# Two expert stages whose tiles without rows run first instead of last, and a shared fill of spare rows

## The chip, the cores and the metric

The kernel runs on one core of a Trainium2 chip. The metric is the device time of one execution in microseconds (us); lower is better. A core has a matrix engine (TensorE, PE in the profile), a vector engine (VectorE, DVE), an activation engine (ScalarE, ACT), a general one (GpSimd, POOL) and an engine that mostly issues transfers (SyncE, SP). Each runs its own list of instructions in order; they wait for each other through semaphores.

## What is computed

Two layers over x of 32 sequences x 128 tokens x 128 channels, so 4096 tokens, in fp32. Both layers end in a mixture of 8 experts of which each token takes two. Cut to what matters here:

```python
def _L0_ffn_ref(x, Wg, W1, W2, W3, Ws1, Ws2, Ws3):      # layer 0, after a per-sequence linear map
    router = xf @ Wg
    top_logits, idx = jax.lax.top_k(router, K)           # K = 2
    probs = jax.nn.softmax(top_logits.astype(jnp.float32), axis=-1).astype(x.dtype)
    w = jnp.zeros((n, E), x.dtype).at[jnp.arange(n)[:, None], idx].add(probs)
    h = jax.nn.silu(jnp.einsum('tc,ech->eth', xf, W1)) * jnp.einsum('tc,ech->eth', xf, W2)
    y = jnp.einsum('eth,ehc,te->tc', h, W3, w)
    hs = jax.nn.silu(xf @ Ws1) * (xf @ Ws2)
    y = y + (hs @ Ws3).reshape(b, t, c)

def _L1_ffn_ref(x, ...):                                 # layer 1, after a per-sequence adapter
    x = x + o @ w_o + b_o                                # o: attention of 16 heads over each sequence
    h = _layernorm(x, ln2_g, ln2_b).reshape(B * S, D)
    topv, topi = jax.lax.top_k(h @ gate_w + gate_b, TOPK)
    hid = jax.nn.relu(jnp.einsum('td,edf->etf', h, W1) + b1[:, None, :])
    out_e = jnp.einsum('etf,efd->etd', hid, W2) + b2[:, None, :]
    moe = jnp.einsum('etd,te->td', out_e, ew)
    return x + moe.reshape(B, S, D)
```

Expert widths are 176 in layer 0 and 512 in layer 1.

## The kernel before, in words

**Stages.** `layer0` routes the tokens and computes the shared part; `experts0` runs layer 0's experts; `pre_attention` and `attention` follow, the latter with layer 1's router; `experts1` runs layer 1's experts and writes the output. Each stage is a block that ends with a barrier of all engines.

**Rows and tiles.** The router gives each pair of token and expert a place in a buffer in memory (`dispatch_rows` in layer 0, `late_rows` in layer 1), where every expert has a region. GpSimd scatters the token rows there with indirect transfers (`route_scatter`, 64 instructions at L358 for each layer). The experts work on tiles of 256 rows. 39 tiles (`ETILES`) always suffice, whatever the routing; a tile beyond those that the routing needs has no rows of tokens. It reads a zeroed dead area, computes on it, and sends its result to spare rows, so it costs what any tile costs. Which expert and which rows a tile takes stands in an integer table that VectorE computes when the routing is over (`table_counts` L420, `table_experts` L439, `table_rows` L449, `table_sends` L460, `table_end` L474): columns 0 to 38 the expert, 39 to 77 the first row, then, from `DONE`, how many sends each half of the result waits for. `w.tabled` is 1 when the experts are there and 2 when the rows are. Tile t takes place t in the list of tiles by expert, so tiles without rows are the last.

Since a region's last tile may be part empty, its tail is filled with spare rows, each from SyncE (`table_fill` L382, with the tile buffer `m.tail` as source): 8 transfers at L389 in layer 0, behind the routing.

**The start of an expert stage.** The first two tiles (`LEAD`) are loaded by SyncE before the stage's block: `lead_weights` (L835) reads the expert number of each from the table (`value_load`, a read of a table entry into a register) and loads its weights; `lead_rows` (L843) reads two row numbers, waits for the tails and for all scatters to have landed, and loads the rows. GpSimd waits for all scatters too, at the end of the preceding block. In the stage SyncE loads tiles 2 to 38 into 8 buffers (`EB`), for each: two table reads (L997, L998), the rows (L1002; L2008 in layer 1), the weights (L1004; L2010).

**In the stage.** Per tile TensorE turns the rows (L889), ScalarE and VectorE split weights and rows in high and low parts (L913, L921 to L925), TensorE multiplies (L939, then L1040 or L2040), ScalarE or VectorE writes the result (`eo` L1094, `fo` L2051), and GpSimd sends it in two indirect transfers (L948, `send_rows`) to `expert_rows`. There are four result buffers (`OB`), each with a semaphore (`st`) that its sends raise.

**The end of an expert stage.** `expert_rows` holds the result for each token twice, for the lower-numbered and for the higher-numbered of its experts. `fetch_halves` (L857) on SyncE, after all loads, fetches the lower half into `V` and the upper one into `X3` (shown as X<-expert_rows), each in four transfers. Ahead of each `sends_done` (L868) reads from the table, for each of the four result buffers, how many sends have to have landed, and waits. The lower half waits for the tiles of experts 0 to 6, the upper half for all tiles that have rows; neither waits for tiles without rows. VectorE adds them: in layer 0 eight lower sums at L956, once all of `V` is there, the upper ones mostly in the next stage; in layer 1 lower and upper ones in turn at L2078 (each upper one waits for its quarter), with the output behind each pair (L2119).

```python
    for b in range(OB):
        at = DONE + OB * a + b
        sends = sp.value_load(m.table[0:1, at:at + 1], min_val=32 * (8 if a else 4), max_val=32 * 10)
        sp.wait_ge(sent[b], sends + 32 * uses(b, OB) if layer else sends)
        sp.sem_inc(m.passed, 1)
```

Of the kernel before, what the change touches and what calls it, by code (L numbers as in the profile page):

```python
# [11 lines left out]
I32 = mybir.dt.int32  # L12
# [4 lines left out]
P = 128  # L17
# [149 lines left out]
def allocate(m, d):  # L167
# [14 lines left out]
    m.table = m.sb("table", [P, DONE + 2 * OB], I32)  # L182
# [12 lines left out]
    m.filled = m.sem("filled")  # L195
# [10 lines left out]
DONE = 2 * ETILES + E  # L206
HALVES = 4
# [155 lines left out]
class TileTable:  # L363
# [3 lines left out]
    def __init__(self, m, ctx, tag, indexed):  # L367
# [8 lines left out]
        self.real, self.sends = sb("real", [P, 2, OB * 10]), sb("sends", [P, 2, OB])  # L376
        self.is_e, self.val, self.val2 = (sb(x, [P, ETILES, E1]) for x in ("is_e", "val", "val2"))
        self.link, self.ended, self.tabled = m.sems(*(s + tag for s in ("tt_link", "ended", "tabled")))
# [14 lines left out]
def table_sync(w, sp):  # L393


    m = w.m
    sp.dma_start(m.xbufs[0][E * REGION:].rearrange("(e a p) c -> p e a c", a=2, p=P), m.tail[:, E:]).then_inc(w.tails, 16)


FILLS = 2  # L400
# [19 lines left out]
def table_counts(w, dve):  # L420
# [12 lines left out]
    c(v.tensor_tensor(w.excl[:], w.incl[:], w.need[:], ALU.subtract))  # L433

# [4 lines left out]
def table_experts(w, dve):  # L439

    m, v, c = w.m, w.m.nc.vector, w.chain
    tl = m.const[:, C_TILE:C_TILE + ETILES]
    c(v.tensor_tensor(w.cmp[:], bc(w.incl[:, 0:E].unsqueeze(1), P, ETILES, E), bc(tl.unsqueeze(2), P, ETILES, E),
# [5 lines left out]
def table_rows(w, dve):  # L449
# [3 lines left out]
    tl = m.const[:, C_TILE:C_TILE + ETILES]  # L453
    c(v.tensor_tensor(w.is_e[:], bc(w.expert[:].unsqueeze(2), P, ETILES, E1), bc(exps.unsqueeze(1), P, ETILES, E1),
                      ALU.is_equal))
    c(v.scalar_tensor_tensor(out=w.val[:], in0=bc(tl.unsqueeze(2), P, ETILES, E1), scalar=float(SLOTS),
# [3 lines left out]
def table_sends(w, dve):  # L460
# [4 lines left out]
    tl = m.const[:, C_TILE:C_TILE + ETILES]  # L465
# [41 lines left out]
def layer0(m, d):  # L507
# [3 lines left out]
    with ExitStack() as ctx:  # L511
# [17 lines left out]
        rank = psN[:, 1, 2 * (P + E):2 * (P + E) + (GT + 1) * E]  # L529
        r = Router(m, ctx, "0", None, ROW_BUFFERS)  # L530
        tiles = TileTable(m, ctx, "0", r.indexed)
        style_ld, first_ld, next_ld, shared_ld, rest_ld, x_ld = m.sems(
# [7 lines left out]
        with nc.Block(no_gpsimd_drain=True) as block:  # L540
            @block.sync
            def _(sp):
# [19 lines left out]
                lead_rows(m, sp, tiles, 16 * (E + 1),  # L562
                          [(r.scattered[b], r.sends * len(range(b, GROUPS, ROW_BUFFERS))) for b in range(ROW_BUFFERS)],
# [3 lines left out]
            def _(pool):  # L567
# [6 lines left out]
                for b in range(ROW_BUFFERS):  # L574
                    pool.wait_ge(r.scattered[b], r.sends * len(range(b, GROUPS, ROW_BUFFERS)))
# [1607 lines left out]
```

## Time and profile before

| | |
|---|---|
| runs of the kernel | 777.63, 775.84, 770.14 us; median 775.84 |
| the profiled execution | 771.82 us, its span 769.0 us |
| busy in the span | PE 80%, DVE 62%, POOL 56%, ACT 50% |
| stage `layer0` | up to about 133 us |
| `experts0` | about 133 to 281 us |
| `pre_attention` and `attention` | about 281 to 603 us |
| `experts1` | about 603 us to the end |
| sends (L948) | 78 in each expert stage, two for each tile |

Times within the profile are counted from the start of the span. A row of the timeline gives start, busy time, engine, line, operation, what is written from what is read, how many like instructions stand in it, and in brackets how long the engine was idle before it and what ended that. SPq and ACTq rows are transfers as the engine issues them; their time is that of issuing. The time of an indirect send is GpSimd's work to issue it; it lands later.

### The profile page before, as it was taken

The numbers are of one execution on the slowest core, as the hardware profiler recorded it, in microseconds if no ns is written. First come the engines' busy times: TensorE is split into PE (matmuls) and PEld (weight loads), VectorE is DVE, ScalarE is ACT, GpSimd is POOL, SyncE is SP. The second block draws the span as 40 slices with busy tenths as digits, with TensorE's granted clock in tenths as the row PEclk, the third lists the DMA queues.
The fourth block names the chain that finished last, engine by engine and source line by source line (L and its number), as shares of the span: only waits on it lengthen the run. The fifth ranks groups of instructions, "written<-read, shape, count | busy, mean of one in ns | idle before, by whom it ended". The sixth has DMA issues, their size and how long they took to land.

```text
span 769.0 us, 17719 instructions
## 1 busy us (share of the span) xinstructions
PE 617.8 (80%) x5541; PEld 490.0 (64%) x5541; DVE 474.6 (62%) x1520; ACT 383.4 (50%) x838; POOL 431.3 (56%) x573
## 2 busy tenths in 40 slices
PE   5797885977778648875999999999972499999882
PEld 2455554977778636552666666666651399999882
DVE  3535344654554556755787787678645477886576
ACT  4323321443444417775767777677632256664441
POOL 2565652455555566634444777877756245664443
PEclk9899988999999957996999999999995599999997
DMA  7999814664656551854493435343101698888747
GB/s 241 221 278 320 236 38 128 187 178 132 169 156 176 169 205 63 249 182 136 126 263 95 130 83 137 93 132 98 43 29 36 209 284 241 249 252 248 209 154 246
DMA packets 106297, 131.21 MB, mean 171 GB/s; under 512 B 16272, under 2 KB 83888, under 8 KB 106096
## 3 DMA queue, kind: packets, MB, share of 16 engines
q1 hardware_dynamic: 92864, 109.40, 50.3%
q0 software_dynamic: 9088, 18.76, 7.0%
q10 hardware_dynamic: 4272, 2.14, 1.0%
q8 instruction: 38, 0.62, 0.3%
q14 instruction: 35, 0.29, 0.1%
HBM read 80.75 MB, written 49.50 MB: 169 GB/s over the span
## 4 chain that ended last, share of the span: by engine, by line
PE 29%; issue 9%; DVE 6%; POOL 5%; another core or an unknown queue 2%; DMA 1%; SPq 1%; ACT 1%; DVEq 0%; POOLq 0%
PE psO L2040 7%; PE psA L939 6%; PE ps L1872 3%; PE psAO L1902 2%; POOL late_rows L358 2%; PE ps L1882 2%; PE ps L1884 2%; PE psAO L1911 2%; PE psT L889 1%; DMA kp<-qk_parts 1%; POOL rstd L1475 1%; DVE mneg L1727 1%; DVE fh L2064 1%; DVE fo L2051 1%
## 5 line engine op out<-in xcount | busy, mean ns | idle before, releaser
L948 POOL DMA_INDIRECT expert_rows<-fo,to x78 | 80.0, 1025 | 78.3 <-DVE fo L2051 53.6
L948 POOL DMA_INDIRECT expert_rows<-eo,to x78 | 77.0, 987 | 76.8 <-ACT eo L1094 59.5
L1727 DVE TENSOR_REDUCE mneg<-ps 128x4 f32<-128x512 f32 x128 | 86.2, 676 | 48.3 <-PE ps L1872 39.7
L1823 ACT ACTIVATE arena<-ps 128x512 f32<-128x512 f32 x128 | 75.3, 589 | 56.3 <-PE ps L1884 55.6
L358 POOL DMA_INDIRECT dispatch_rows<-row,index x64 | 62.8, 982 | 54.4 <-DVE index L339 37.4
L939 PE MATMUL psA<-xh,wh 128*128 128x256 f32 (+1 forms) x234 | 73.7, 315 | 15.6 <-DVE xl L925 15.0
L921 DVE CAST xh<-psT 128x256 fp32r<-128x256 f32 x78 | 32.7, 420 | 79.6 <-PE psT L889 38.9
L358 POOL DMA_INDIRECT late_rows<-row,index x64 | 64.0, 1000 | 20.3 <-issue 15.1
L1872 PE MATMUL ps<-km,qp 96*128 96x512 f32 x128 | 63.5, 502 | 10.9 <-ACT km L1816 7.3
L1816 ACT ACTIVATE km<-kp,const 96x512 fp32r<-96x512 f32 x96 | 67.8, 713 | 8.3 <-PEq L1180 4.6
L939 PE MATMUL psA<-xh,wl 128*128 128x256 f32 (+1 forms) x234 | 67.1, 287 | 0.0
L939 PE MATMUL psA<-xl,wh 128*128 128x256 f32 (+1 forms) x234 | 67.1, 287 | 0.0
L1662 POOL TENSOR_SCALAR km<-kp,const 96x512 fp32r<-96x512 f32 x32 | 50.1, 1564 | 19.9 <-POOLq L1180 13.7
L2040 PE MATMUL psO<-wb,fh 128*128 128x128 f32 x464 | 57.9, 279 | 1.9 <-issue 1.9
L2040 PEld LDWEIGHTS psO<-wb,fh 128*128 128x128 f32 x464 | 55.8, 196 | 2.1 <-issue 2.1
L939 PEld LDWEIGHTS psA<-xh,wh 128*128 128x128 f32 (+1 forms) x234 | 42.8, 183 | 19.4 <-DVE xl L925 18.3
L1882 PE MATMUL ps<-qm,kp 96*128 96x512 f32 x128 | 52.0, 406 | 1.7 <-ACT arena L1823 1.5
L1884 PE MATMUL ps<-mxT,selr 128*128 128x512 f32 x128 | 51.2, 400 | 0.0
L939 PEld LDWEIGHTS psA<-xl,wh 128*128 128x128 f32 (+1 forms) x234 | 43.0, 184 | 0.2 <-issue 0.2
L939 PEld LDWEIGHTS psA<-xh,wl 128*128 128x128 f32 (+1 forms) x234 | 42.9, 183 | 0.0
L1872 PEld LDWEIGHTS ps<-km,qp 96*128 96x128 f32 x128 | 25.5, 201 | 25.6 <-issue 16.4
L1060 DVE TENSOR_TENSOR eh<-psB,es 88x512 f32<-88x512 f32 x39 | 26.6, 683 | 22.1 <-PE psB L939 16.4
(227 smaller groups left out, 1591.0 us busy)
## 6 DMA issues: line engine op xcount, KB each, us to landing
late_rows<-tail SPq DMA_DIRECT2D x17, 1040.0 KB
wb<-in_W1b SPq DMA_DIRECT2D x29, 578.0 KB
w<-in_W SPq DMA_DIRECT2D x29, 304.0 KB
qk_parts<-qk SPq DMA_DIRECT2D x8, 1024.0 KB, 4.6
qp<-qk_parts SPq DMA_DIRECT2D x48, 128.0 KB
kp<-qk_parts SPq DMA_DIRECT2D x48, 128.0 KB
qm<-qk_parts SPq DMA_DIRECT2D x192, 32.0 KB
arena<-in_W1b SPq DMA_DIRECT2D x10, 578.0 KB
```

Of the source, the lines that this page charges most:

```text
L358: pool.indirect_dma_start(out=r.xbuf, out_offset=bass.IndirectOffsetOnAxis(ap=r.index[b][:, c:c + 1], axis=0), in_=r.row[b][:, c // TOPK, ...
L921: v.tensor_copy(z.xh[q][:], z.psT[:, q, 0:SLOTS]).then_inc(z.x_high, 1)
L939: ins = z.m.nc.tensor.matmul(out, w[k][q][:, columns], x[k][q][:], start=(k == 0), stop=(k == 2), skip_group_check=True)
L948: pool.indirect_dma_start(out=m.ybuf, out_offset=bass.IndirectOffsetOnAxis(ap=to[b][:, a:a + 1], axis=0), in_=out[b][:, a, :], in_offset=N ...
L1662: ins = nc.gpsimd.tensor_scalar(km[s % 2][:, :, j, :], kp[side(s)][:, :, tok(s)].bitcast(F32), mask(j), None, ALU.mult)
L1727: nc.vector.tensor_reduce(mneg[s % 2][:, g, :], ps1[:, g % 2, :].rearrange("p (j k) -> p j k", j=4), AX_X, ALU.max, negate=True).then_inc( ...
L1816: nc.scalar.activation(km[s % 2][:, :, j, :], kp[side(s)][:, :, tok(s)].bitcast(F32), ACT.Copy, scale=mask(j)).then_inc(km_act, 1)
L1823: nc.scalar.activation(prob[s % 2][:, g, :], ps2[:, g % 2, :], ACT.Exp, scale=ATT_SCALE).then_inc(exped, 1)
L1872: nc.tensor.matmul(ps1[:, g % 2, :], qp[side(s)][:, g, tok(s)], km[s % 2][:, g].rearrange("p j k -> p (j k)"), start=True, stop=True).then ...
L1882: nc.tensor.matmul(ps2[:, g % 2, :].rearrange("p (j k) -> p j k", j=4), kp[side(s)][:, g, tok(s)], qm[(s // 2) % 2][:, g, :, tok(s)], star ...
L1884: nc.tensor.matmul(ps2[:, g % 2, :], selr[:, g, :], mxT[s % 2][:].rearrange("p j k -> p (j k)"), start=False, stop=True).then_inc(shifted, 1)
L2040: ins = nc.tensor.matmul(psO[:, q, a * P:(a + 1) * P], h[q][:, k, a * P:(a + 1) * P], wb[b][:, WIDE + k * P:WIDE + (k + 1) * P], start=(k ...
```

## The change

- `table_counts` computes for tile t the place (t + R) mod 39, where R is the number of tiles that the routing needs. Tiles without rows (39 - R of them) come first, those with rows last, in the order of before.
- The table has new entries: for tiles 2 to 8 (`FIRST_REAL`) the value 2 or 3 of `tabled` for which a tile's row load waits, and for each landing semaphore (`LEAD_WAIT`, four in layer 0, two in layer 1) how much of it the lead tiles need: all of it if tile 1 has rows, else only one transfer.
- `lead_rows` waits for the dead area's fill, reads and waits for each landing entry, and then reads each row number just ahead of its load. GpSimd no longer waits for the scatters at the end of `layer0` and `attention`; it does so at the start of the expert stage (`rows_landed`), and raises `tabled` to 3.
- In both expert stages SyncE issues a tile's weights ahead of its rows, and tiles 2 to 7 read (2 to 6) and wait (2 to 7) for `tabled` between the two.
- `sends_done` for the upper half waits for the sends of all 39 tiles, without table reads; the lower half's counts contain the tiles without rows, which now run first.
- Four of the eight tail fills of layer 0 go from SyncE to ScalarE's queue, behind ScalarE's work of the stage.

```diff
@@ table_counts
+    c(v.tensor_tensor(w.raw[:], m.const[:, C_TILE:C_TILE + ETILES], bc(w.incl[:, E - 1:E], P, ETILES), ALU.add))
+    c(v.tensor_scalar(w.wrap[:], w.raw[:], float(ETILES), float(-ETILES), ALU.is_ge, ALU.mult))
+    c(v.tensor_tensor(w.place[:], w.raw[:], w.wrap[:], ALU.add))
@@ table_sends
-    tl = m.const[:, C_TILE:C_TILE + ETILES]
+    v.tensor_scalar(w.wrap[:], w.raw[:], float(-ETILES), None, ALU.add)
     c(v.memset(w.real[:], 0.0))
+    ins = v.tensor_scalar(m.table[:, FIRST_REAL:FIRST_REAL + EB - 1], w.wrap[:, 0:EB - 1], 0.0, 2.0, ALU.is_ge, ALU.add)
+    if w.layer == 0:
+        ins.then_inc(w.tails, 1)
+    for k, (sem, total, least) in enumerate(m.landing[w.layer]):
+        v.tensor_scalar(m.table[:, LEAD_WAIT + k:LEAD_WAIT + k + 1], w.wrap[:, LEAD - 1:LEAD], 0.0, float(total - least),
+                        ALU.is_ge, ALU.mult)
     for a in range(2):
-        ins = v.tensor_tensor(w.real[:, a, 0:ETILES], tl, bc(w.incl[:, E - 2 + a:E - 1 + a], P, ETILES), ALU.is_lt)
+        ins = v.tensor_tensor(w.real[:, a, 0:ETILES], w.wrap[:], bc(w.incl[:, E - 2 + a:E - 1 + a], P, ETILES), ALU.is_lt)
@@ layer0, SyncE, GpSimd and ScalarE
-                table_fill(tiles, sp, range(E))
+                table_fill(tiles, sp, range(TAIL_ACT, E))
...
-                for b in range(ROW_BUFFERS):
-                    pool.wait_ge(r.scattered[b], r.sends * len(range(b, GROUPS, ROW_BUFFERS)))
...
+                table_fill(tiles, act, range(TAIL_ACT))
@@ lead_rows and what is new beside it
+def when_there(m, sp, layer, n):
+    ready = sp.value_load(m.table[0:1, FIRST_REAL + n:FIRST_REAL + n + 1], min_val=2, max_val=3)
+    sp.wait_ge(m.tabled[layer], ready)
+    sp.sem_inc(m.passed, 1)
+
+def lead_rows(m, sp, layer, dead, xs):
+    sp.wait_ge(m.tabled[layer], 2)
+    sp.wait_ge(*dead)
+    for k, (sem, total, least) in enumerate(m.landing[layer]):
+        more = sp.value_load(m.table[0:1, LEAD_WAIT + k:LEAD_WAIT + k + 1], min_val=0, max_val=total - least)
+        sp.wait_ge(sem, more + least)
+        sp.sem_inc(m.passed, 1)
     for b in range(LEAD):
-        sp.dma_start(xs[b], xbuf[bass.ds(rows[b], SLOTS), :].rearrange("(a p) c -> p a c", p=P)).then_inc(m.ld[b], 16)
+        row = sp.value_load(m.table[0:1, b + ETILES:b + ETILES + 1], min_val=0, max_val=E * REGION + (E - 1) * SLOTS)
+        sp.dma_start(xs[b], m.xbufs[layer][bass.ds(row, SLOTS), :].rearrange("(a p) c -> p a c", p=P)).then_inc(m.ld[b], 16)
+
+def rows_landed(m, pool, layer):
+    for sem, total, least in m.landing[layer]:
+        pool.wait_ge(sem, total)
+    pool.sem_inc(m.tabled[layer], 1)
@@ sends_done
     for b in range(OB):
-        at = DONE + OB * a + b
-        sends = sp.value_load(m.table[0:1, at:at + 1], min_val=32 * (8 if a else 4), max_val=32 * 10)
+        if a:
+            sp.wait_ge(sent[b], 32 * uses(b, OB) * (layer + 1))
+            continue
+        sends = sp.value_load(m.table[0:1, DONE + b:DONE + b + 1], min_val=32 * 4, max_val=32 * 10)
@@ experts0, SyncE (experts1 alike, with its own table semaphore)
+                    sp.dma_start(w[b][:], d["W123"][bass.ds(e, 1)].rearrange("e p h -> (e p) h")).then_inc(ld[b], 16)
+                    if isinstance(n, int) and n < EB - 1:
+                        when_there(m, sp, 0, n)
+                    elif isinstance(n, int) and n < EB:
+                        sp.wait_ge(m.tabled[0], 3)
                     sp.dma_start(xs[b][:], m.xbufs[0][bass.ds(row, SLOTS), :].rearrange("(a p) c -> p a c", p=P)
-                                 ).then_inc(ld[b], 16)
-                    sp.dma_start(w[b][:], d["W123"][bass.ds(e, 1)].rearrange("e p h -> (e p) h")
                                  ).then_inc(ld[b], 16)
```

The order of SyncE's instructions in layer 0, from the lead tiles' rows on; TENSOR_LOAD is a table read, ISA and REGISTER_ALU are the small instructions around it, `rt_scattered0_*` and `tails0` the landing semaphores. Before:

```order
L848 TENSOR_LOAD table [waits tabled0]
L848 ISA x2
L848 TENSOR_LOAD table
L848 ISA x2
L854 ISA [waits rt_scattered0_1,rt_scattered0_2,rt_scattered0_0,tails0]
L854 DMA lead_xs<-dispatch_rows 128x2x130
L854 ISA
L854 DMA lead_xs<-dispatch_rows 128x2x130
```

In the changed kernel (L873 is the landing reads, L877 and L878 the row reads and loads):

```order
L873 TENSOR_LOAD table [waits dead_in,tabled0]
L873 ISA x2
L874 REGISTER_ALU
L873 TENSOR_LOAD table [waits rt_scattered0_0]
...
L877 TENSOR_LOAD table [waits tails0]
L877 ISA x2
L878 ISA
L878 DMA lead_xs<-dispatch_rows 128x2x130
L877 TENSOR_LOAD table
L877 ISA x2
L878 ISA
L878 DMA lead_xs<-dispatch_rows 128x2x130
```

The one wait for everything became four pairs of read and wait, and five table reads stand ahead of the first row load, where there were two. The waits themselves are for less.

SyncE in layer 1's stage, from behind the last tile's loads to the end. Before (L873 is the read of `sends_done`, `e_st*` the semaphores of the result buffers):

```order
L865 DMA V<-expert_rows 128x1024 [waits e_st3]
L865 DMA V<-expert_rows 128x1024 x3
L873 TENSOR_LOAD table
L873 ISA x2
L874 REGISTER_ALU
L873 TENSOR_LOAD table [waits e_st0]
...
L865 DMA X<-expert_rows 128x1024 [waits e_st3]
L865 DMA X<-expert_rows 128x1024 x3
```

In the changed kernel:

```order
L907 TENSOR_LOAD table [waits e_st2]
L907 ISA x2
L908 REGISTER_ALU
L897 DMA V<-expert_rows 128x1024 [waits e_st3]
L897 DMA V<-expert_rows 128x1024 x3
L897 DMA X<-expert_rows 128x1024 [waits e_st2,e_st3,e_st1,e_st0]
L897 DMA X<-expert_rows 128x1024 x3
```

Between the two fetches the four reads are gone, and the upper fetch waits for all four buffers' sends at constants.

## Rows read from the trace of the kernel before

**Rows 1.** Stretches: busy time of each engine, instruction groups, clock, DMA share, GB/s.

```profile
140.00:257.00 117.00, 94.98 (x757) 90.00 (x755) 62.51 (x166) 52.92 (x133) 64.84 (x66) 0.97 0.58 166
274.00:278.00 4.00, 0.00 (x0) 0.00 (x0) 4.00 (x8) 0.00 (x0) 1.94 (x2) 0.50 1.01 399
620.00:690.00 70.00, 70.00 (x614) 70.00 (x613) 57.16 (x166) 41.92 (x102) 43.60 (x41) 1.00 0.86 254
690.00:735.00 45.00, 40.01 (x339) 38.58 (x338) 29.60 (x89) 22.01 (x56) 20.68 (x22) 1.00 0.74 223
```

**Rows 2.** Timeline of SyncE's queue, start of layer 0's expert stage.

```profile
130.54 0.96 SPq L854 DMA_DIRECT2D lead_xs<-dispatch_rows  x2
134.16 0.37 SPq L1002 DMA_DIRECT2D xs<-dispatch_rows  x1
...
149.25 0.35 SPq L1002 DMA_DIRECT2D lead_xs<-dispatch_rows  x1
```

**Rows 3.** Timeline of GpSimd, VectorE and TensorE, the same place.

```profile
121.64 0.96 POOL L358 DMA_INDIRECT dispatch_rows<-row,index  x1 [0.31 <-issue]
...
128.00 0.52 DVE L479 TENSOR_REDUCE table<-val 128x39 int32<-128x351 f32 x1
...
133.50 0.73 PE L889 MATMUL psT<-const,lead_xs 128*128 128x128 f32 x3 [1.75 <-DMA lead_xs<-dispatch_rows]
```

**Rows 4.** Waits from 140 to 257: us in total, times, longest.

```profile
ACT wh L913 <- DMA w<-in_W: 10.7, 10, 1.8
...
PE psT L889 <- DMA w<-in_W: 6.4, 7, 2.8
...
PE psT L889 <- DMA lead_w<-in_W: 5.4, 5, 1.9
```

**Rows 5.** Timelines of SyncE's queue, GpSimd and VectorE, end of layer 0's stage.

```profile
265.45 1.41 SPq L865 DMA_DIRECT2D V<-expert_rows  x4
270.26 1.29 SPq L865 DMA_DIRECT2D X<-expert_rows  x4
...
259.68 0.96 POOL L948 DMA_INDIRECT expert_rows<-eo,to  x1 [0.30 <-issue]
...
269.55 1.36 POOL L948 DMA_INDIRECT expert_rows<-eo,to  x1 [0.30 <-issue]
...
273.54 4.96 DVE L956 TENSOR_TENSOR X<-V,X 128x512 f32<-128x512 f32 x8 [0.86 <-DMA V<-expert_rows]
```

**Rows 6.** Timeline, start of layer 1's stage.

```profile
601.43 0.96 POOL L358 DMA_INDIRECT late_rows<-row,index  x1 [0.30 <-issue]
...
606.37 1.14 PE L889 MATMUL psT<-const,arena 128*128 128x128 f32 x4 [15.60 <-DMA arena<-late_rows]
```

**Rows 7.** Chain that ended last, the same place: start, us, what.

```profile
598.01 0.27 SPq L848
...
598.56 0.29 SPq L848
...
599.62 4.23 issue
...
604.04 2.28 DMA arena<-late_rows
```

**Rows 8.** Timeline of GpSimd, layer 1's stage after 692 us.

```profile
699.53 0.96 POOL L948 DMA_INDIRECT expert_rows<-fo,to  x1 [3.36 <-DVE fo L2051]
...
707.93 0.95 POOL L948 DMA_INDIRECT expert_rows<-fo,to  x1 [3.54 <-DVE fo L2051]
```

**Rows 9.** Timeline, end of layer 1's stage.

```profile
749.82 0.95 POOL L948 DMA_INDIRECT expert_rows<-fo,to  x1 [0.30 <-issue]
...
752.13 1.76 SPq L865 DMA_DIRECT2D X<-expert_rows  x4
...
757.18 0.73 DVE L2078 TENSOR_TENSOR X<-X 128x512 f32<-128x512 f32 x1
...
759.72 0.96 POOL L948 DMA_INDIRECT expert_rows<-fo,to  x1 [0.30 <-issue]
```

More of the change, by code:

```diff
@@ L181, in allocate @@
     m.tail = m.sb("tail", [P, 2 * E, 2, ROW])
-    m.table = m.sb("table", [P, DONE + 2 * OB], I32)
+    m.table = m.sb("table", [P, LEAD_WAIT + LANDINGS], I32)
     m.styles = m.sb("styles", [P, SEQS])
@@ L206 @@
 DONE = 2 * ETILES + E
+FIRST_REAL = DONE + 2 * OB
+LEAD_WAIT = FIRST_REAL + EB - 1
+LANDINGS = 4
 HALVES = 4
@@ L376, in __init__ @@
         self.real, self.sends = sb("real", [P, 2, OB * 10]), sb("sends", [P, 2, OB])
+        self.raw, self.wrap, self.place = (sb(x, [P, ETILES]) for x in ("raw", "wrap", "place"))
         self.is_e, self.val, self.val2 = (sb(x, [P, ETILES, E1]) for x in ("is_e", "val", "val2"))
-        self.link, self.ended, self.tabled = m.sems(*(s + tag for s in ("tt_link", "ended", "tabled")))
+        self.link, self.tabled = m.sems(*(s + tag for s in ("tt_link", "tabled")))
+        self.ended = m.sem("ended0") if tag == "0" else m.passed
+        self.layer = int(tag)
+        m.tabled[self.layer] = self.tabled
         self.tails = m.sem("tails0") if tag == "0" else m.filled
@@ L396, in table_sync @@
     m = w.m
-    sp.dma_start(m.xbufs[0][E * REGION:].rearrange("(e a p) c -> p e a c", a=2, p=P), m.tail[:, E:]).then_inc(w.tails, 16)
+    sp.dma_start(m.xbufs[0][E * REGION:].rearrange("(e a p) c -> p e a c", a=2, p=P), m.tail[:, E:]).then_inc(m.dead_in, 16)
+TAIL_ACT = 4
 FILLS = 2
@@ L529, in layer0 @@
         rank = psN[:, 1, 2 * (P + E):2 * (P + E) + (GT + 1) * E]
+        sb("apart", [P, 2 * GW])
         r = Router(m, ctx, "0", None, ROW_BUFFERS)
         tiles = TileTable(m, ctx, "0", r.indexed)
+        m.landing[0] = [(r.scattered[b], r.sends * len(range(b, GROUPS, ROW_BUFFERS)), 16) for b in range(ROW_BUFFERS)]
+        m.landing[0].append((tiles.tails, 16 * E + 1, 1))
         style_ld, first_ld, next_ld, shared_ld, rest_ld, x_ld = m.sems(
@@ L559, in _ @@
                     fill_region(m, sp, e)
-                table_fill(tiles, sp, range(E))
+                table_fill(tiles, sp, range(TAIL_ACT, E))
                 lead_weights(m, sp, tiles, d["W123"], [w[:] for w in m.lead_w])
-                lead_rows(m, sp, tiles, 16 * (E + 1),
-                          [(r.scattered[b], r.sends * len(range(b, GROUPS, ROW_BUFFERS))) for b in range(ROW_BUFFERS)],
-                          m.xbufs[0], [x[:] for x in m.lead_xs])
+                lead_rows(m, sp, 0, (m.dead_in, 16), [x[:] for x in m.lead_xs])
             @block.gpsimd
@@ L1112, in _ @@
             def _(pool):
+                rows_landed(m, pool, 0)
                 for n, b, i in rounds(pool, ETILES, EB, head=EB, tail=EB - 1):
@@ L1624, in attention @@
         tiles = TileTable(m, ctx, "1", post.router.indexed)
+        m.landing[1] = [(sem, post.router.sends * GROUPS // 2, 16) for sem in post.router.scattered]
         mask = lambda j: m.const[0:96, C_MASK + j:C_MASK + j + 1]
@@ L1651, in _ @@
                 lead_weights(m, sp, tiles, d["W1b"], m.late_w)
-                lead_rows(m, sp, tiles, 16 * (FILLS * E + 1),
-                          [(sem, post.router.sends * GROUPS // 2) for sem in post.router.scattered], m.xbufs[1], m.late_xs)
+                lead_rows(m, sp, 1, (m.filled, 16 * (FILLS * E + 1)), m.late_xs)
             @block.gpsimd
@@ L1715, in _ @@
                 pool.wait_ge(post.joined, GROUPS)
-                for b in range(2):
-                    pool.wait_ge(post.router.scattered[b], post.router.sends * GROUPS // 2)
             @block.vector
```

25 lines of the change are left out of this document (10 added, 15 removed).

## The prediction

> **What bounds the kernel now.** I read the profile in the order in which the stages run, and asked at each stage's two ends what came last, since the change moves tiles only inside the two expert stages. The table of stretches first [rows 1]: from 620 to 690 us the second expert stage is TensorE's, 70.00 us busy of 70, with 614 groups of matmuls, 8.8 per us. From 690 to 735 it has 339 in 45 us, 7.5 per us, and is idle for 5.0 us. So inside layer 1's stage no order of tiles can gain anything before 690; what can move is its start, its end and those 5 us.
>
> The first expert stage is not TensorE's: from 140 to 257 it is busy 94.98 of 117 us [rows 1], and among its waits are 10.7 us of ScalarE, in 10 pieces, for weights from memory [rows 4]. Its start is SyncE's: two row loads at 130.54, then tile 2's at 134.16 [rows 2]. The last scatter there starts at 121.64, nine us ahead of the row loads [rows 3]: **the landing of the scatters is not what layer 0's first tiles wait for.** VectorE ends the table at 128.52 (128.00 + 0.52), and TensorE turns tile 0 at 133.50 [rows 3].
>
> The start of layer 1's stage is different: in the chain of what ended last [rows 7] the table is there when SyncE reads the first row number at 598.01; it has both by about 599.1, and then 4.23 us are "issue", a semaphore wait. The last scatter starts at 601.43 and ends at 602.39 [rows 6]; the row loads go at 604.04 and land 2.28 us later [rows 7], with TensorE behind them at 606.37 [rows 6]. Here the landing of the scatters sets the start.
>
> **How many tiles have no rows.** The reference's routing of the given inputs fills 12, 1, 1, 1, 16, 2, 1 and 2 tiles in layer 0 and 0, 4, 4, 4, 2, 6, 4 and 12 in layer 1: 36 of 39 in both. The trace bears out layer 1. The upper fetch there goes at 752.13 [rows 9], and the last send of the fourth-last tile (number 35 of 0 to 38) starts at 749.82 and ends at 750.77, so 1.35 us lie between a send's end and the fetch it frees. The three tiles after it were not waited for. In the changed kernel tiles 0, 1 and 2 are without rows, so both lead tiles are, and neither of them waits for scatters.
>
> **Part 1, layer 0's start.** The table needs three more chained operations of 39 columns (an estimate of 0.2 us each: the table's last one, on 351 columns, takes 0.52 [rows 3]) and some unchained ones; the row numbers are there at about 129.1, not 128.52. SyncE then reads a number from the table and waits, four times for the landings, and reads the first tile's row: five reads where the old code had two ahead of the first load. The price of one read with its wait: at least 0.55 (598.01 to 598.56, from one read to the next) [rows 7], at most 0.85 ((270.26 - 265.45 - 1.41)/4, the four reads between two fetches) [rows 5]. I take 0.73. 129.1 + 5 x 0.73 = 132.7 against 130.54 for the first row load: +2.2. Tile 0's start moves by +1.9 to +2.2. Then tiles 2 to 6 each have one more read, five times 0.7 or so, on the queue which in this stretch issues a tile each 2.5 us (tiles 2 to 8, 134.16 to 149.25) [rows 2]; by tile 8 SyncE is +5 or so late. The stage's pace behind that is up to 3.7 us a tile (149.25 to the fetch at 265.45 for 31 tiles) [rows 2, 5], so some of this is slack; I take two us. ScalarE's half of the tails takes four issues from SyncE's queue; but the lead weights behind them wait for the table, so this gives nothing. Sum: **+3**, bounds 0 (all slack) and +5 (none). Weights go out ahead of rows now, 0.56 us earlier per tile; it shortens the waits of [rows 4] once per round of eight buffers, 4 x 0.56 at most; it is inside those bounds.
>
> **Part 2, layer 0's end.** The lower fetch waits for all tiles of experts 0 to 6: 34 tiles before (0 to 33), and 3 + 34 = 37 now (0 to 36). The last send of tile 33 starts at 259.68 and ends at 260.64; the fetch went at 265.45, 4.8 later [rows 5]. Tile 36's ends at 270.91 (269.55 + 1.36). With the 1.35 landing and the three reads that stand behind it on SyncE (its semaphore is the first of four) that is 274.5; with the old 4.8 it is 275.7. So V goes out 9.0 to 10.3 later. VectorE waits for all of V, 8.1 us after its issue (273.54 - 265.45), and has been idle for just 0.86 us then: nothing hides a later V. The eight lower sums of 4.96 and the stage's end stand behind it. One us may come back, since V shares the transfers with nothing of X. **+9**, bounds 8 and 11. The upper fetch waits for the last tile, two behind, lands behind V and is hidden by the lower sums.
>
> **Part 3, layer 1's start.** The table's row numbers now come at about 598.95 (598.01 and about 0.9 for the added operations). Two landing reads and a row read, 3 x 0.7: the row load goes at 601.1 and lands 2.28 later, 603.4, where TensorE began at 606.37 [rows 6, 7]. GpSimd's last scatter ends at 602.39 and the stage begins after it, so 603.0 is a floor. **-2.9**, bounds -1.5 and -3.4. TensorE then runs at its own pace [rows 1], so all of it is kept, until the end.
>
> **Part 4, layer 1's end.** The upper fetch now waits for the last send of the last tile: it starts at 759.72 and ends at 760.68, and with 1.35 the fetch goes at 762.03 instead of 752.13 [rows 9]. A quarter of 512 KB lands after about 3.2 us: 2.28 of a 130 KB load [rows 7] and the remaining 382 KB at the 399 GB/s of 274 to 278 us [rows 1]. First upper sum at 765.2 instead of 757.18; the 14 sums from there to the end, and the output behind them, are unchanged. **+8**, bounds 7 and 10.5. The lower fetch waits for tile 26, long done when SyncE gets there: nothing.
>
> The trace has 1.35 us from a send's end to the fetch behind it [rows 9]. The Trainium skill (DMA: Bandwidth & Descriptors, Anatomy of one DMA, SWDGE path) gives such a transfer a fixed cost of about 2.0 us, nearly all behind the issue, and a small part by bytes: by it an estimate would put the last fetch 0.8 us later and the sum at +18. The sum goes by the trace.
>
> **Sum.** +3 + 9 - 2.9 + 8 = +17.1 on a profiled execution of 771.82 us (span 769.0): 788.9. That execution lies 4.0 below the median of 775.84, so on the median it would be 793. The three runs shown lie 7.5 apart, so I forecast between the two: 791.
>
> **The rivals.**
> A. *The sends bunch up in more of layer 1.* After 692 us the sends of GpSimd go out four in a row, once per 8.4 us (699.53, 707.93) [rows 8], and in this stretch TensorE is idle for 5.0 us [rows 1]. Per two tiles 8.4 stands against 6.84 (70 us for 614 groups, 30 a tile). If another phase of the tiles brings this on earlier, each tile costs 0.5 to 0.8 more, and half of the 24 free tiles give +6 to +10: 797 to 801, all of them 810. Against it: it did not happen from 620 to 690.
> B. *The starts are absorbed, or those 5 us vanish.* Layer 0's +3 is slack, or the bunching goes: -3 to -6, 782 to 787.
> C. *The other side: layer 0 loses its waits for weights.* Weights first is what would do it. ScalarE's 10.7 and TensorE's 6.4 and 5.4 for weights are 22.5 us [rows 4]; were they in series and all gone, 771.8 + 17.1 - 22.5 = 766. It decides only from 17 of the 22.5 up. Against it: an earlier issue by 0.56 cannot add up tile by tile, since SyncE itself waits for buffers to come free.
> D. *The ends cost nothing.* If the tiles without rows were fewer than I count, or the end's fetch waits not so long as read, starts and ends would nearly cancel: within 1%.
>
> **How the numbers follow.** The forecast 0.62, with its own range of 785 to 797; A 0.14; B 0.12; C 0.04; D 0.08. The range of 781 to 803 holds the forecast, B and most of A. Slower by over 1% (about what a measurement of this kernel can tell from none) is the forecast, A and B, 0.88; within 1% is D less 0.01, 0.07; faster is C and that 0.01, 0.05.
>
> **What would show it.** Layer 0: the first lead row load near 132.7, tile 8's near 153, the V fetch 9 later than the stage's start shift, VectorE idle about 9 us for V where it was 0.86. Layer 1: the lead row load 3 us after the table instead of 6; TensorE still full to 690; the X fetch behind the last send, and an idle VectorE of 6 to 8 us ahead of the first upper sum. Wrong would be: a V fetch that waits for SyncE's own queue instead of sends, a pace in layer 0 other than that of before, or sends in fours from the start of layer 1.

## The result, and the profile after

The changed kernel takes 795.15 us (median of 4 runs, 790.53 to 798.69) against 774.23 us of the kernel before, run beside it: a ratio of 1.0278, 95% interval 1.0237 to 1.0319, or about 21 us more. The forecast was 791, and 17 us more. Ratios, here and below, leave out executions in a slower state that this chip shows at times: two of the kernel before, and three of the changed machinery without the turn, its profiled one among them. The profiled execution has a span of 793.3 us where it was 769.0; from the page:

```profile
span 793.3 us, 17774 instructions
PE 615.9 (78%) x5541; PEld 486.4 (61%) x5541; DVE 477.3 (60%) x1536; ACT 384.0 (48%) x838; POOL 433.3 (55%) x573
```

Busy times are those of before within 4 us on each engine, so the 24 us between the two spans are nearly all waits (the medians lie 21 apart; the profiled pair shows the difference 3 us too large). Where they lie is read from like instructions in both traces; worked out from their times, in us:

```
                                                before    after    more
table's end to layer 0's first row load           2.02     3.81    +1.8
first turn of layer 0 (time)                    133.50   131.75    -1.8
first turn to the end of the last send          142.84   145.65    +2.8
last send's end to the end of the stage           4.74    13.53    +8.8
end of the stage to the end of the last scatter 321.31   323.96    +2.6
last scatter's end to layer 1's first turn        3.99     4.30    +0.3
first turn to the fifth cast of rows (xh)        12.80    15.63    +2.8
fifth cast to the end of the last send          141.50   141.53     0.0
last send's end to the end of the kernel          8.31    16.97    +8.7
```

The two ends make 17.5 of it. The first row is no term of its own, since it lies ahead of the first turn. The timelines of SyncE's queue, GpSimd and VectorE at the end of layer 0's stage, after (L982 is the send, L897 the fetch, L990 the lower sums):

```profile
270.34 1.45 POOL L982 DMA_INDIRECT expert_rows<-eo,to  x1 [0.30 <-issue]
...
275.42 1.81 SPq L897 DMA_DIRECT2D V<-expert_rows  x4
282.83 1.74 SPq L897 DMA_DIRECT2D X<-expert_rows  x4
...
284.28 4.91 DVE L990 TENSOR_TENSOR X<-V,X 128x512 f32<-128x512 f32 x8 [10.71 <-DMA V<-expert_rows]
...
290.94 0.99 POOL L1270 MEMSET aT<- 128x512 f32 x2 [13.53 <-POOLq L1025]
```

The send at 270.34 is the last of tile 36. The V fetch goes 3.6 us behind its end, and VectorE stands for 10.71 us where it stood 0.86 [rows 5]; the lower sums start 10.7 us later than at 273.54. At the end of layer 1's stage:

```profile
775.40 0.96 POOL L982 DMA_INDIRECT expert_rows<-fo,to  x1 [0.30 <-issue]
...
777.75 1.74 SPq L897 DMA_DIRECT2D X<-expert_rows  x4
...
781.68 0.69 DVE L2118 TENSOR_TENSOR X<-X 128x512 f32<-128x512 f32 x1 [8.09 <-DMA X<-expert_rows]
...
788.91 1.29 DVE L2118 TENSOR_TENSOR X<-X 128x512 f32<-128x512 f32 x2
```

Before, the fetch went 8.55 us ahead of the end of the last send [rows 9] and lay under the last tiles; now it goes 1.4 behind it, and VectorE waits 8.09 us, where no wait stood before its first upper sum [rows 9].

The start of layer 1's stage was to give 2.9 us back. It did not in this trace (L495 ends the table, L856 and L878 are the lead loads):

```profile
609.40 2.83 SPq L856 DMA_DIRECT2D arena<-in_W1b  x2
...
610.97 0.52 DVE L495 TENSOR_REDUCE table<-val 128x39 int32<-128x351 f32 x1
...
613.93 0.96 POOL L362 DMA_INDIRECT late_rows<-row,index  x1 [0.31 <-issue]
616.96 1.52 SPq L878 DMA_DIRECT2D arena<-late_rows  x2
...
619.20 0.69 PE L923 MATMUL psT<-const,arena 128*128 128x128 f32 x2 [15.95 <-DMA arena<-late_rows]
```

From the table's end at 611.49 to the first row load are 5.5 us, for which I had three table reads and 2.1. SyncE was still at the second lead weight load until 612.22, and only then came to the reads. The load waits for no scatter, and still goes two us behind the last one, as before [rows 6, 7].

### The profile page after: what moved, and what is told of

Same layout as the page of the kernel before. It is cut to its first block and busy times, and to the rows that moved or that the text cites. A ratio compares the mean times of both kernels' runs of the same rounds, so it can differ in the third digit from the quotient of the medians.

```text
span 793.3 us, 17774 instructions
## 1 busy us (share of the span) xinstructions
PE 615.9 (78%) x5541; PEld 486.4 (61%) x5541; DVE 477.3 (60%) x1536; ACT 384.0 (48%) x838; POOL 433.3 (55%) x573
## 5 line engine op out<-in xcount | busy, mean ns | idle before, releaser
L982 POOL DMA_INDIRECT expert_rows<-fo,to x78 | 80.5, 1033 | 80.9 <-DVE fo L2091 57.7
L982 POOL DMA_INDIRECT expert_rows<-eo,to x78 | 77.1, 988 | 77.0 <-ACT eo L1131 59.3
L973 PE MATMUL psA<-xh,wh 128*128 128x256 f32 (+1 forms) x234 | 74.7, 319 | 10.3 <-DVE xl L959 8.8
L1852 ACT ACTIVATE km<-kp,const 96x512 fp32r<-96x512 f32 x96 | 67.8, 713 | 12.2 <-PEq L1218 6.4
L973 PEld LDWEIGHTS psA<-xh,wh 128*128 128x128 f32 (+1 forms) x234 | 43.7, 187 | 12.5 <-DVE xl L959 11.3
L1097 DVE TENSOR_TENSOR eh<-psB,es 88x512 f32<-88x512 f32 x39 | 26.7, 685 | 24.4 <-PE psB L973 17.2
```

The lines of the kernel that those rows point to most:

```text
L973: ins = z.m.nc.tensor.matmul(out, w[k][q][:, columns], x[k][q][:], start=(k == 0), stop=(k == 2), skip_group_check=True)
L982: pool.indirect_dma_start(out=m.ybuf, out_offset=bass.IndirectOffsetOnAxis(ap=to[b][:, a:a + 1], axis=0), in_=out[b][:, a, :], in_offset=N ...
L1852: nc.scalar.activation(km[s % 2][:, :, j, :], kp[side(s)][:, :, tok(s)].bitcast(F32), ACT.Copy, scale=mask(j)).then_inc(km_act, 1)
```

## The experiments

The twelve kernels below ran in three groups of four, each group on a chip of its own with the kernel before beside it, and are compared with that alone. Of the chips that they ran on, two give that kernel 704 to 707 us and not 770; what differs there is told at the end.

My theory: the loss is the wait of the two end fetches for sends that now come last, and not the machinery (reads, load order, fills). The rival: the machinery costs it, or the turned order of experts does.

**The turned table alone.** The kernel before, with `place` for the tile number in the table (and `raw` less 39 where sends are counted), and nothing else:

```diff
+    c(v.tensor_tensor(w.raw[:], m.const[:, C_TILE:C_TILE + ETILES], bc(w.incl[:, E - 1:E], P, ETILES), ALU.add))
+    c(v.tensor_scalar(w.wrap[:], w.raw[:], float(ETILES), float(-ETILES), ALU.is_ge, ALU.mult))
+    c(v.tensor_tensor(w.place[:], w.raw[:], w.wrap[:], ALU.add))
...
-    tl = m.const[:, C_TILE:C_TILE + ETILES]
+    tl = w.place[:]
```

> The kernel before with the table rotated (tiles without rows first) and nothing else: lead rows, load order, fills and end waits stay in the code of before. If the ends carry the loss, the V fetch of layer 0 goes about 10 us later and the first upper sum of layer 1 about 8.6 us later against the last sends: +17 to +18 us, ratio 1.022 to 1.024. If the extra reads and waits on SyncE carry most of it, it is at most +8 us, ratio under 1.011.

Measured: 1.0207 (1.0169 to 1.0244), or 16 us, a little under the range I gave. The fetch that waits, with the send that it waits for, in layer 0 (tile 36's) and in layer 1 (the last tile's):

```profile
270.82 0.96 POOL L953 DMA_INDIRECT expert_rows<-eo,to  x1 [0.30 <-issue]
...
275.04 1.79 SPq L870 DMA_DIRECT2D V<-expert_rows  x4
...
283.46 4.91 DVE L961 TENSOR_TENSOR X<-V,X 128x512 f32<-128x512 f32 x8 [9.11 <-DMA V<-expert_rows]
...
766.08 0.96 POOL L953 DMA_INDIRECT expert_rows<-fo,to  x1 [0.30 <-issue]
769.07 1.74 SPq L870 DMA_DIRECT2D X<-expert_rows  x4
773.05 0.69 DVE L2083 TENSOR_TENSOR X<-X 128x512 f32<-128x512 f32 x1 [8.77 <-DMA X<-expert_rows]
```

From the last send's end to the end of the stage it takes 12.2 us in layer 0, 17.6 in layer 1, against 4.7 and 8.3. That is +16.8 of ends, and leaves nothing of the 16 us to explain.

**The machinery without the turn.** The changed kernel with `place` equal to the tile number and the upper fetch's counts read as before:

```diff
-    c(v.tensor_tensor(w.place[:], w.raw[:], w.wrap[:], ALU.add))
+    c(v.tensor_copy(w.place[:], m.const[:, C_TILE:C_TILE + ETILES]))
```

> The changed kernel with the place of tile t put back to t, so that tiles without rows are last again, and the upper fetch waiting as before for tiles with rows; all reads, the load order, ScalarE's fills and GpSimd's moved wait stay. By the theory of the ends: +2 to +5 us (reads at both starts), ratio 1.003 to 1.006, with the first tiles of layer 1 about 3 us later against the last scatter. If the machinery carries the loss: over +12 us, ratio over 1.015.

Measured: 1.0037 (0.9997 to 1.0076), about 3 us and hardly clear of nothing. The rival, at over 12 us, falls. One part of the expectation missed: layer 1's first turn comes 4.6 us behind the last scatter, where it was 4.0 before and 4.3 in the changed kernel, and not 3 us later.

**Only the last wait.** The kernel before, with the upper fetch waiting for all 39 tiles:

```diff
+        if a:
+            sp.wait_ge(sent[b], 32 * uses(b, OB) * (layer + 1))
+            continue
```

> The kernel before, with only the upper fetch's wait changed to the sends of all 39 tiles. By the theory of the ends: layer 1's first upper sum moves from 757.2 to about 765.7, +8.5 us, and layer 0's stage end by +2 to +3 since the upper rows then land behind the lower sums; ratio 1.012 to 1.015. If the 8.6 us at the end came from something else (rows order, the contention of output transfers): under +4 us, ratio under 1.005.

Measured: 1.0176 (1.0112 to 1.0240), above the range I gave. Its four times fall in two pairs, 777.4 and 777.7, 785.7 and 787.2; what parts them is open. The profile is of the lower pair and bears the numbers of the expectation out: layer 0's end 7.1 us behind the last send (+2.4), layer 1's 17.2 (+8.9). Timeline of its last send and fetch:

```profile
757.69 0.96 POOL L951 DMA_INDIRECT expert_rows<-fo,to  x1 [0.30 <-issue]
...
760.04 1.74 SPq L865 DMA_DIRECT2D X<-expert_rows  x4
```

The tiles are in their old order here; the wait alone makes the whole of layer 1's end.

**Without the reads of tiles 2 to 6.** The changed kernel, with a constant in place of each:

```diff
-    ready = sp.value_load(m.table[0:1, FIRST_REAL + n:FIRST_REAL + n + 1], min_val=2, max_val=3)
-    sp.wait_ge(m.tabled[layer], ready)
-    sp.sem_inc(m.passed, 1)
+    sp.wait_ge(m.tabled[layer], 3)
```

> The changed kernel with the five table reads of tiles 2 to 6 replaced by a constant wait for the third count (the rows of all tiles landed). If the reads slow the first eight tiles of both stages, layer 1's stage gets back about 2.8 us between its first tile and tile 3, and layer 0's up to 2: ratio to before 1.021 to 1.025, 3 to 5 us under the changed kernel. If the prologue's lag is something else (weights ahead of rows), no difference: 1.027.

Measured: 1.0155 (1.0126 to 1.0185), below the 1.021 to 1.025 I expected. Its profiled span of 784.2 us is that of the turned table alone (784.7), and its ends are those of the changed kernel (13.1 and 17.2 us behind the last sends). In layer 0 the stage from first turn to last send took 142.6 us, as before (142.8) and not the 145.7 of the changed kernel, so on this sort of chip the reads may well cost those 2.8 us; on the other sort the changed kernel takes 114.4 with them, and the kernels of its group 113.9 to 115.9 without. Layer 1's first turn to the fifth cast took 12.7 us, not 15.6. But that does not convict the reads of layer 1: the changed kernel on another chip took 13.1 with them, and the kernel with layer 0 alone turned took 15.8 without them. What differs is TensorE's clock. Stretches of 3 us in the changed kernel, from the second one after layer 1's first turn on (after the span: busy time of PE, PEld, DVE, ACT, POOL, then granted clock, DMA share, GB/s):

```profile
622.40:625.40 3.00, 2.30 (x12) 2.01 (x11) 1.10 (x4) 1.30 (x3) 0.00 (x0) 0.50 0.84 251
625.40:628.40 3.00, 3.00 (x16) 3.00 (x15) 1.59 (x5) 1.10 (x4) 0.00 (x0) 0.50 0.84 245
628.40:631.40 3.00, 3.00 (x20) 3.00 (x19) 0.73 (x3) 0.76 (x2) 0.00 (x0) 0.65 0.86 259
631.40:634.40 3.00, 3.00 (x28) 3.00 (x27) 2.73 (x8) 1.81 (x5) 0.85 (x1) 1.00 0.85 259
```

and in the kernel before:

```profile
609.40:612.40 3.00, 3.00 (x16) 3.00 (x16) 1.31 (x5) 1.47 (x3) 0.00 (x0) 0.50 0.92 289
612.40:615.40 3.00, 3.00 (x27) 3.00 (x27) 2.17 (x6) 1.41 (x3) 0.00 (x0) 0.96 0.92 301
```

TensorE stays at 0.50 (1.2 GHz) for 11.3 us after its first turn at 619.2, against 6.3 us after 606.4: five more us at half the clock, which is 2.5 us of work and nearly the 2.8. In the second stretch it was idle for 0.70 of 3 us, where before it was busy throughout. In the kernel with layer 0 alone turned the same two things stand together. In this one the clock is back in the second stretch, idle or not:

```profile
616.40:619.40 3.00, 2.62 (x17) 2.42 (x17) 1.47 (x6) 1.47 (x3) 0.00 (x0) 0.76 0.98 330
619.40:622.40 3.00, 3.00 (x28) 3.00 (x28) 1.87 (x6) 1.69 (x4) 0.00 (x0) 1.00 0.92 273
```

In the fourteen profiles the clock is back 4.7 to 8.3 us after the first turn where the fifth cast comes after 12.5 to 13.9 us, and only in these two kernels after 11.3 and 11.5, where the cast comes after 15.6 and 15.8. So the 2.8 us go with the clock, they come or stay out from kernel to kernel, and what settles it is open.

**One tile first, two last.** A turn by one instead of three:

```diff
+    c(v.tensor_scalar(w.ahead[:], m.const[:, C_TILE:C_TILE + ETILES], -1.0, None, ALU.add))
+    c(v.tensor_scalar(w.below[:], w.ahead[:], 0.0, float(ETILES), ALU.is_lt, ALU.mult))
+    c(v.tensor_tensor(w.place[:], w.ahead[:], w.below[:], ALU.add))
```

> The kernel before with the list of places turned by one: one tile without rows first, two last. If the loss is the wait of the end fetches for late sends, it must follow the number of tiles put behind: the V fetch of layer 0 waits for tile 34, not 33 (+0 to +2.5), and layer 1's upper fetch for tile 36, whose last send ends 2.6 us after tile 35's, of which VectorE's own queue ahead of the first upper sum hides 1.8 us: in all +1 to +4 us, ratio 1.001 to 1.005, against +16 for three tiles. If the turned table itself costs (its operations, the other order of experts), it is +8 or more, ratio over 1.010.

Measured: 1.0103 (1.0060 to 1.0146), 7 us, well over the 1 to 4 I gave, and by the ratio inside the range that I had given to the rival (the table itself costs). The trace decides between them: from the last send's end it takes 8.3 us to the end of layer 0's stage and 14.0 to the end of layer 1, against 5.7 to 6.6 and 9.5 in the kernels of this sort of chip with an untouched end. That is +1.7 to 2.6 and +4.5, which leaves one us at most. Its last fetch, with tile 36's last send ahead of it:

```profile
691.81 0.96 POOL L952 DMA_INDIRECT expert_rows<-fo,to  x1 [0.30 <-issue]
...
696.21 1.74 SPq L869 DMA_DIRECT2D X<-expert_rows  x4
...
700.95 0.69 DVE L2082 TENSOR_TENSOR X<-X 128x512 f32<-128x512 f32 x1 [4.54 <-DMA X<-expert_rows]
```

The fetch goes 3.4 us behind the send's end, not 1.4: tile 36's semaphore is the first of four, and three table reads stand behind its wait. I had used that for layer 0 and left it out here. VectorE waits 4.5 us for one tile put behind, and 8.1 for three. The loss grows with the number of tiles, as the theory says, but its price begins with the reads.

**Rows ahead of weights.** The changed kernel, with `lead_rows` called before `lead_weights` in layer 1:

```diff
-                lead_weights(m, sp, tiles, d["W1b"], m.late_w)
                 lead_rows(m, sp, 1, (m.filled, 16 * (FILLS * E + 1)), m.late_xs)
+                lead_weights(m, sp, tiles, d["W1b"], m.late_w)
```

> The changed kernel, with lead_rows ahead of lead_weights in the stage before layer 1's experts. If SyncE's instructions crawl (0.7 us each) because its two 578 KB weight loads are under way, they do not crawl now and the first row load goes about 2.1 us after the table's end, not 5.5; but the weights then land later, so TensorE's first turn comes at most 3 us earlier against the last scatter: ratio 1.021 to 1.026. If the crawl has another cause, the row load still goes 5 us after the table's end, and the weights 3 us later still: 1.027 to 1.031.

Measured: 1.0272 (1.0235 to 1.0309), over the 1.021 to 1.026 I gave. The start of its stage:

```profile
555.72 1.60 SPq L878 DMA_DIRECT2D arena<-late_rows  x2
555.77 0.96 POOL L362 DMA_INDIRECT late_rows<-row,index  x1 [0.30 <-issue]
...
558.10 1.45 SPq L856 DMA_DIRECT2D arena<-in_W1b  x2
...
562.27 0.69 PE L923 MATMUL psT<-const,arena 128*128 128x128 f32 x2 [16.90 <-DMA arena<-in_W1b]
```

The row load goes 2.4 us behind the table's end, but the weights are now last and TensorE turns 5.5 us behind the last scatter. It does not show the weight loads guilty of the slow reads, for on a chip of this sort the changed kernel too needs only 2.2 us (below).

**The four fills on ScalarE alone**, on the kernel before:

```diff
-                table_fill(tiles, sp, range(E))
+                table_fill(tiles, sp, range(TAIL_ACT, E))
...
+                table_fill(tiles, act, range(TAIL_ACT))
```

> The kernel before with only the four tail fills moved to ScalarE's queue. By the theory: the row load of layer 0's first tile waits for table and SyncE's reads, so it moves by under 1.5 us, ratio 0.996 to 1.003. If the fills on SyncE's queue had held the start up, the first turn comes 2 to 3 us earlier: ratio 0.996 or less.

Measured: 0.9993 (0.9971 to 1.0015). Nothing, on the second sort of chip.

**Weights ahead of rows alone**, each tile's two loads in both stages of the kernel before turned round:

> The kernel before with only the order of each tile's two loads turned (weights, then rows) in both stages. By the theory: within 2 us, ratio 0.997 to 1.003, the first turn of a stage unchanged. By the rival that weights issued late bound layer 0: its stage from first turn to last send (142.8 us before) gets 5 us or more shorter, ratio under 0.994.

Measured: 0.9998 (0.9979 to 1.0016). Nothing, so such waits as those for weights [rows 4] are not to be had by their order. This ran on the second sort of chip, and [rows 4] are from the first; there the changed kernel has the same order, and its stage of layer 0 got no shorter (145.7 us from first turn to last send, 142.8 before).

**Each layer's turn alone.** The turned table of the first experiment, in one layer and not in the other (VectorE's added operations run in both):

```diff
+        self.turned = tag == "0"
...
+    tl = w.place[:] if w.turned else m.const[:, C_TILE:C_TILE + ETILES]
```

> The kernel before with the turned table in layer 0 alone. By the theory of the ends the V fetch waits for tile 36 instead of 33 and all of layer 0's loss is there: stage end minus the last send's end grows from 4.7 to 12 or 13 us, +7 to +9 in all, ratio 1.009 to 1.013. By the rival that the turned order costs throughout (other experts' weights, crawling SyncE): over +12.

> The kernel before with the turned table in layer 1 alone: the time from the last send's end to the end grows from 8.3 to about 17 us, +8 to +9.5, ratio 1.010 to 1.013; the two single ones add up to the ratio of both (1.0207). By the rival: the stage itself, from first turn to last send, gets longer than the 153 to 154 us of before.

Measured: 1.0094 (1.0074 to 1.0114) for layer 0 and 1.0114 (1.0086 to 1.0142) for layer 1. The sum is 1.0208, and both together had 1.0207, though on the other sort of chip. Layer 0 alone, its end:

```profile
225.54 1.07 POOL L954 DMA_INDIRECT expert_rows<-eo,to  x1 [0.30 <-issue]
...
229.94 1.85 SPq L871 DMA_DIRECT2D V<-expert_rows  x4
...
238.26 4.91 DVE L962 TENSOR_TENSOR X<-V,X 128x512 f32<-128x512 f32 x8 [9.88 <-DMA V<-expert_rows]
...
244.92 0.99 POOL L1238 MEMSET aT<- 128x512 f32 x2 [12.91 <-POOLq L997]
```

Layer 1 alone, its end:

```profile
691.70 0.96 POOL L954 DMA_INDIRECT expert_rows<-fo,to  x1 [0.30 <-issue]
694.70 1.74 SPq L871 DMA_DIRECT2D X<-expert_rows  x4
...
698.90 0.69 DVE L2084 TENSOR_TENSOR X<-X 128x512 f32<-128x512 f32 x1 [8.40 <-DMA X<-expert_rows]
```

On this sort of chip the kernels with an untouched end need 5.7 to 6.6 us from layer 0's last send to its stage's end, and 9.5 to the end of layer 1; these two need 12.9 and 17.9. The rival's sign is absent: with layer 1 turned, its stage from first turn to last send takes 143.8 us, with layer 1 as before 142.8 to 146.1.

**All four reads, then all four waits**, at the end fetches of the kernel before:

```diff
+    sends = []
     for b in range(OB):
         at = DONE + OB * a + b
-        sends = sp.value_load(m.table[0:1, at:at + 1], min_val=32 * (8 if a else 4), max_val=32 * 10)
-        sp.wait_ge(sent[b], sends + 32 * uses(b, OB) if layer else sends)
+        sends.append(sp.value_load(m.table[0:1, at:at + 1], min_val=32 * (8 if a else 4), max_val=32 * 10))
+    for b in range(OB):
+        sp.wait_ge(sent[b], sends[b] + 32 * uses(b, OB) if layer else sends[b])
         sp.sem_inc(m.passed, 1)
```

> The kernel before, in which the end fetches read all four send counts first and then wait four times. The V fetch of layer 0 goes 1.4 us sooner behind tile 33's landing, more where SyncE's instructions crawl (up to 3 us, as 265.5 for a semaphore that was up at 262.4 allows), nothing in layer 1: -1 to -3 us, ratio 0.996 to 1.000. If the reads behind the waits are hidden: 1.000.

Measured: 1.0000 (0.9982 to 1.0017), and not 1 to 3 us less. A read with its wait takes some 0.7 us on this chip. The fetch did move: V goes 1.6 us behind the end of tile 33's last send, and 3.5 and 4.2 in the two kernels with other loads alone changed, and VectorE waits 1.8 us for it and not 3.2 and 4.8. But V then lands 10.3 us after its issue and not 9.2 and 8.8, and the whole time shows nothing of it. I had hoped that it would beat the kernel before; nothing tried here does.

**The changed kernel once more**, beside the last three:

> The changed kernel once more, beside the single parts on one chip. By the theory it is the sum of the ends (about +17) and of the reads at both starts, less what the tiles without rows save at layer 1's start: ratio 1.022 to 1.028. If SyncE does not crawl on this chip, layer 1's row load goes 2 to 3 us after the table's end, not 5.5, the first turn 2 us earlier against the last scatter, and the lag between the first turn and the fifth cast (2.8 us in the first trace) is 1 us or less.

Measured: 1.0210 (1.0144 to 1.0276). The start of its layer 1:

```profile
548.58 0.52 DVE L495 TENSOR_REDUCE table<-val 128x39 int32<-128x351 f32 x1
...
551.29 1.58 SPq L878 DMA_DIRECT2D arena<-late_rows  x2
551.54 0.96 POOL L362 DMA_INDIRECT late_rows<-row,index  x1 [0.30 <-issue]
...
554.34 0.69 PE L923 MATMUL psT<-const,arena 128*128 128x128 f32 x2 [13.22 <-DMA arena<-late_rows]
```

The ratio is a little under the 1.022 to 1.028 I gave. Here the gain of the change is to be seen: the row load goes 2.2 us behind the table's end and ahead of the last scatter, and TensorE's first turn comes 1.8 us behind that scatter's end, where the kernels that wait for all scatters need 4.1 to 4.7. The mechanism works and is worth 2.3 to 2.9 us there; the ends, 13.4 and 17.1 us behind the last sends, cost some 15, five to six times that. In the whole time the gain is not to be seen: the ratio of 1.0210 is that of the two turned tables (1.0208), and its interval of 0.0066 either way is wider than the gain.

## Why the prediction was right, point by point

**Sign, size and main cause: right.** Slower, by the end fetches' waits. Layer 0's end, forecast at +9, was +8.8 in the trace. Layer 1's, forecast at +8, was +8.7; the mis-sized term is the landing of the first quarter, 3.2 us by my sum and 3.9 measured (777.75 to 781.68), while the 1.35 us between send and fetch held (1.4). From the end of GpSimd's issue to the fetch the trace has 1.4 us in the changed kernel and in the one that only waits for all. The Trainium skill (DMA: Bandwidth & Descriptors, Anatomy of one DMA, SWDGE path) gives such a transfer a fixed cost of about 2.0 us, setup included. I had counted that from the end of the issue, and it does not hold so; counted from its start (775.40 to 777.75) the trace has 2.35 us, and the page is near it.

**Layer 0's start: the price right, the sum too high.** Five reads ahead of the first row load took 3.81 us from the table's end, as the 3.65 of five times 0.73 said. But the table itself came 2.8 us sooner, not 0.6 later (ahead of its last operations VectorE stood 6.45 us for a releaser that the trace cannot name before, and 2.30 us for TensorE after), so the first turn came 1.8 us sooner and not 2 later. From first turn to tile 8's load it was 20.5 us instead of 15.8, +4.8 where my sum had some 3; tile 8's load came at 152.26, near the 153 forecast. Of these 4.8 us 2.8 were left at the last send, so the slack was the two us I took. In all the last send came 1.1 us later, where the sum had +3. As the tables of the six profiles of this sort of chip end from 123.96 to 129.01, the early table may be chance, and no single profile settles that term. That two errors, the table and the pace, work against each other here is luck.

**Layer 1's start: the failed step.** "Two landing reads and a row read, 3 x 0.7" and the -2.9 that rested on it. The mechanism is right, as the changed kernel's second run shows (2.3 to 2.9 us won); on the chip of the first traces the row load went 5.5 us behind the table's end, and nothing was gained. I had taken the price of a read from stretches in which SyncE ran freely, although the trace of before has others: tile 38's loads there went at 256.06 and 257.47, 1.41 us apart, for what takes 0.56 elsewhere.

**Two terms were missing.** TensorE's slower return to full clock (+2.8), and +2.6 between the stages. Whether the latter is part of the change is open: the same stretch takes 316.8 to 321.4 us in the other kernels of this sort of chip, turned or not, and 324.0 in the changed one; on the second sort it is 309.4 in the changed kernel and 310.1 with rows ahead of weights, and 307.5 to 308.9 in the rest. No run separates it. On the profiled executions, +24.3 against +17.1: 5.4 for these two, 3.2 for layer 1's start, 0.5 for the ends, less 1.9 for layer 0's start. By the medians I was 4 us low.

**The rivals.** Bunching of the sends in more of layer 1 (A) did not come: TensorE was busy 70.00 of 70 us from 630 to 700, and the first pause ahead of four sends stands at the stage's 47th send in both kernels, at 699.53 before [rows 8] and at 715.24 after. The other side (C) is refuted by the result itself, whose layer 0 has weights first and is no shorter, and on the second sort of chip by the load order alone, 0.9998. That the ends cost nothing (D) is refuted by each kernel with a turned table.

## What to carry to other kernels

Work without use belongs where nobody waits for what follows it. Here that was the end: the last tiles covered the landing of the sends and the fetch behind them, 7 to 9 us a stage, while at the start they could at best cover the landing of the scatters, 2 to 3 us in layer 1. Before moving filler from one end of a stage to the other, sum what each end's chain would wait for without it. And a semaphore read by a register costs 0.7 us for each read that stands behind the wait that comes last: ask which of several waits that is.

## What the runs showed that I had not expected

**Two sorts of chips.** The same kernel before has a median of 769.4 us beside one group of experiments, 707.1 and 704.0 beside the two others. Each chip had one group, at one time, so I cannot tell a trait of the chip from one of the hour. In the first sort's traces SyncE's small instructions come in steps of about 0.7 us for stretches at a time, with 34 to 52 that took 0.65 to 0.75 us in each trace; in the second sort's there are 1 to 4. At the start of layer 1 in the changed kernel the two landing reads make six such steps from 612.23 to 616.52 (load, register, wait), where the second sort has some 1.4 us. With the weight loads that came late by the same pace, that makes 5.5 us of 2.2. VectorE and ScalarE have their part: from 700 to 750 us of the changed kernel

```profile
DVE xh L955 <- remote: 15.3, 5, 3.1
...
ACT fw L2140 <- remote: 9.2, 3, 3.2
```

are waits whose releaser the trace does not know, VectorE's five of some 3 us, one in each group of four sends; the kernel before has the same, with 15.0 us in five from 690 to 740. In the second sort's traces VectorE has no wait over 2.5 us there. Layer 0's stage takes 114 to 118 us from first turn to last send in them, not 142 to 151, and layer 1's fifth cast to last send 129.6 to 131.0, not 140 to 141.5. I take both for engines that wait for their own instructions, which fits steps of one length on several engines; this is argued and not shown, and the queues of instruction transfers in the trace do not bear it out: in the kernel before they carry nothing from 664 to 719 us, while three of the five waits end between 696 and 714. What is shown is that the bunching that I priced as a rival is not a matter of the order of the tiles: in the traces of the first sort it begins at the 47th send, turned or not, and in those of the second sort it is absent.

The start of layer 0 is another one too. On the first sort the row load goes 2.0 us behind the table's end in the kernel before; in the second sort's kernels with the old start it goes 14 to 19 us behind it, and not for the table: with layer 1 alone turned, SyncE has the row numbers at 110.06, and its wait for tails and scatters is over at 113.49. The changed kernel, whose first tiles wait for less, has 10.0 us there; the four fills on ScalarE alone did not do it (18.8). TensorE's first turn gains only 0.3 to 1.3 us of that against the kernels of its group.

**The ratio hardly knows the chip.** 1.0278 on one sort and 1.0210 on the other for the changed kernel. The ends cost 17.5 us on the first and some 15 on the second, 2.1 to 2.3% of the time on both. The start's gain shows in the trace of the second sort alone, but the two intervals meet, and that it makes the rest of the difference is not shown.
